# Row one-hots of a graph network's first norm: one broadcast comparison of two tensors, or 17 comparisons with a per-partition scalar

## The reference

```
h = relu(layernorm(x))                         # first norm
x = x + segment_sum(mlp(h[src], h[dst]), src)  # 128 -> 128 -> 128 -> 64, softplus
h = relu(layernorm(x))                         # second norm
z = relu((h + segment_sum(h[src], dst)) @ W1 + b1) @ W2 + b2
x = x + h + relu(batchnorm(z))
```

## Time and profile before

| | |
|---|---|
| three runs | 1983.5, 1985.07, 1986.97 us; median 1985.07 |
| the profiled execution | 1981.82 us, of which the span from first to last instruction is 1979.3 us |
| `prepare`, first `row_hot` to last | 82.17 to 289.41 us of the span, 49 blocks |
| DVE busy | 1063.9 us of the span, 3259 instructions |
| POOL busy | 1071.2 us of the span, 1151 instructions |
| PE busy | 1428.0 us |
| mean granted TensorE clock | 0.894 |

### The profile page before, as it was taken

One profiled execution on the slowest core, in us unless ns is written; L12 is line 12 of the kernel. 1 busy time (PEld: TensorE's weight loads), 2 busy tenths in 40 slices (PEclk: granted clock), 3 DMA queues, 4 the chain that ended last, 5 costly groups with the idle time before them and its releaser, 6 DMA issues. The chain is left out here.

```text
span 1979.3 us, 37799 instructions
## 1 busy us (share of the span) xinstructions
PE 1428.0 (72%) x10165; PEld 1067.5 (54%) x10165; DVE 1063.9 (54%) x3259; ACT 975.3 (49%) x2310; POOL 1071.2 (54%) x1151
## 2 busy tenths in 40 slices
PE   0033337999999999999999994666556556566566
PEld 0022225777777777777777784443434334334334
DVE  4899993555555555555555555443443433433344
ACT  0188885776777777677777763111111111111144
POOL 0388884454444445445444542776666666666600
PEclk9999999999999999999999997777777777777765
DMA  1255544444554554455455453222222222222259
GB/s 34 61 125 130 122 109 115 125 119 119 130 129 110 128 135 115 122 129 127 111 129 136 111 138 73 58 57 55 47 53 51 50 54 46 54 54 46 33 180 340
DMA packets 435913, 200.77 MB, mean 101 GB/s; under 512 B 382585, under 2 KB 408710, under 8 KB 435866
## 3 DMA queue, kind: packets, MB, share of 16 engines
q1 hardware_dynamic: 343384, 142.00, 27.7%
q0 software_dynamic: 28224, 32.57, 9.1%
q10 hardware_dynamic: 64258, 25.65, 4.5%
HBM read 131.49 MB, written 55.79 MB: 95 GB/s over the span
## 5 line engine op out<-in xcount | busy, mean ns | idle before, releaser
L821 POOL DMA_INDIRECT fast_gathered<-h_table,fast_gather_i x441 | 423.2, 960 | 471.8 <-PE bank L963 295.0
L1180 POOL DMA_INDIRECT fast_gathered<-h_neighbours_table,fast_index_i x441 | 425.8, 966 | 197.4 <-POOL fast_index_i L1176 104.9
L1080 ACT ACTIVATE fast_h<-bank,b_s 128x384 f32<-128x384 f32 (+1 forms) x490 | 299.7, 622 | 177.7 <-PE bank L990 140.4
L1241 PE MATMUL node_sums<-twice,fast_self_rows 128*64 128x128 f32 x784 | 139.0, 423 | 279.3 <-DMA fast_gathered<-h_neighbours_table,fast_index_i 275.2
L1241 PEld LDWEIGHTS node_sums<-twice,fast_self_rows 128*64 128x64 f32 x784 | 120.5, 222 | 317.5 <-issue 307.0
L1272 ACT ACTIVATE fast_z_in<-node_sums 128x512 f32<-128x512 f32 x49 | 29.3, 597 | 517.7 <-PE node_sums L1247 517.7
L1087 ACT ACTIVATE fast_h<-fast_h 128x384 f32<-128x384 f32 (+1 forms) x490 | 263.8, 558 | 0.0
L1226 DVE BATCH_NORM_STATS2 z_stats<-z_t (+1 forms) x48 | 33.3, 694 | 386.2 <-ACT z_t L1283 386.2
L999 PE MATMUL bank<-fast_h,w_s 128*128 128x384 f32 (+1 forms) x490 | 235.3, 562 | 2.8 <-ACT fast_h L1087 1.9
L1247 PE MATMUL node_sums<-fast_hot,fast_gathered 128*64 128x256 f32 (+1 forms) x980 | 217.4, 444 | 0.0
L1034 PE MATMUL node_sums<-fast_message,fast_hot 128*128 128x80 f32 x1568 | 200.9, 276 | 0.0
(11 more groups left out here) (234 smaller groups left out, 2578.9 us busy)
## 6 DMA issues: line engine op xcount, KB each, us to landing
fast_local<-local_rows SPq DMA_DIRECT2D x49, 576.0 KB, 5.5
h_neighbours_table<-fast_h_rows SPq DMA_DIRECT2D x49, 320.0 KB
fast_self_rows<-h_neighbours_table SPq DMA_DIRECT2D x49, 320.0 KB, 3.3
h_table<-prep_normed ACTq DMA_DIRECT2D x49, 256.0 KB, 2.7
fast_own_rows<-h_table SPq DMA_DIRECT2D x49, 256.0 KB
fast_own_cols<-h_cols SPq DMA_DIRECT2D x49, 256.0 KB
x_plus_h<-fast_total SPq DMA_DIRECT2D x49, 256.0 KB, 6.4
finish_resid<-x_plus_h SPq DMA_DIRECT2D x49, 256.0 KB, 4.0
```

The source lines that it names most:

```text
L821: pool.indirect_dma_start(gathered[slot][:, j * D:(j + 1) * D], None, h0_t, bass.IndirectOffsetOnAxis(ap=gather_i[q][:, n:n + 1], axis=0))\
L1080: A(to[at][:, 0:w], psum[:, 0:w], ACT.Exp, bias=b_s[:, :]).then_inc(done, 1)
L1180: pool.indirect_dma_start(gathered[q][:, c * MW:(c + 1) * MW], None, h1_t, bass.IndirectOffsetOnAxis(ap=index_i[q][:, c:c + 1], axis=0))\
L1241: nc.tensor.matmul(banks[6 + q % 2][h * D:(h + 1) * D, k * P:(k + 1) * P], self_rows[q][:, at:at + D], twice[:, :], start=(k == 0), stop=F ...
```

## The change

In `row_hots` the one comparison of two broadcast views (17 x 128 elements per partition) becomes 17 comparisons of `iota_h` (128 elements) with one number per partition, field 1 of the n-th edge. The result is the same tensor. The semaphore that tells of it moves to the last of the 17. Nothing else is changed, no wait and no DMA; 16 x 49 = 784 instructions are added on VectorE.

```diff
@@ -566,10 +566,10 @@
                                             iota_tile[:, bass.ds(b * CT, CT)].unsqueeze(1).to_broadcast([128, RAW, CT]),
                                             ALU.is_equal).then_inc(tile_hot_ready, 1)
                             wait_from(dve, pack_done, b - 1)
-                            V.tensor_tensor(groups(row_hot[q % 2][:, :], P),
-                                            f[:, :, 1:2].to_broadcast([128, RAW, P]),
-                                            iota_h[:, :].unsqueeze(1).to_broadcast([128, RAW, P]),
-                                            ALU.is_equal).then_inc(row_hot_ready, 1)
+                            for n in range(RAW):
+                                last = V.tensor_scalar(row_hot[q % 2][:, n * P:(n + 1) * P], iota_h[:, :],
+                                                       f[:, n, 1:2], None, ALU.is_equal)
+                            last.then_inc(row_hot_ready, 1)
```

## The result

The changed kernel took 2055.07 us (median of 4 runs, 2053.63 to 2055.91) against 1984.28 us before on the same chip (4 runs): a ratio of 1.0354, 95% interval 1.0336 to 1.0372, slower. The profiled execution took 2054.45 us, its span 2049.4 us.

The account below looks back on a forecast made before the run. VectorE was taken to set prepare's pace, 4.32 us a block, in a round with GpSimd where each waits for the other. +0.38 + 1.41 - 0.37 = +1.42 us a block, x 49 = +70 us, gave 2055 us, range 2000 to 2090.

Parts of the forecast that it names:

- The chain: In prepare, 17 comparisons at 0.16 us, 2.72 us, replace row_hot's 2.34: +0.38 us a block (-0.30 to +0.89).
- the two ends: Limits for one comparison in prepare: 0.12 us with elements free, 0.19 with elements as dear as four-byte ones.
- GpSimd gets in: Inside prepare's 17 comparisons, spread and centre get in and VectorE stands: +1.41 us a block.
- the first hold: In prepare, spread holds VectorE 0.84 us, less 0.12 fixed; centre's hold of 0.69 follows, with nothing taken off.
- Given back: In prepare, centre_rest no longer meets centre, falling from 0.65 to 0.28 us: -0.37 us a block.
- The sum: In prepare, +0.38 + 1.41 - 0.37 = +1.42 us a block, x 49 = +70 us.
- B: In prepare, GpSimd is kept out until the 17th comparison; only the chain is longer: 2004 us, chance 0.17.
- C: In prepare, the new comparisons share nothing with GpSimd, so no stall is left: 1985.5 us, chance 0.12.
- D: In prepare, the scalar's price vanishes (0.10 us each) and GpSimd is kept out or not met: 1960 us, chance 0.07.
- E: The change fails its purpose, for instance scalars 10 bytes apart cost another 0.06 us each: 2105 us, chance 0.04.

Follow-up runs that it names:

- the probe: Kernel before plus scratch-writing VectorE chains in setup, alone and beside GpSimd subtractions: 0.165 us per comparison with two-byte scalar; ten beside GpSimd took 2.37 us, not 1.63.
- the kernel before with the same wait: Kernel before, with GpSimd's spread made to wait until row_hot is through: 1997.6 us, ratio 1.006.

## Why the prediction was right

**The chain.** I forecast +0.38 us a block, and +0.42 was found (2.76 - 2.34): 0.1625 us from start to start where I took 0.16 from rows of four-byte numbers. No row had two-byte numbers in and out, so the middle between the two ends was a choice; it was right because the elements cost 0.033 us, as the probe shows. The probe also shows the scalar's load at 0.06 us. By the formula of the Trainium skill's page "VectorE: DVE Perf Modes", section "The TRN2 errata", the estimate is 0.094 us each. The probe agrees with it for a constant in the instruction (0.10 us) and not for a scalar per partition (0.163).

**GpSimd gets in.** I forecast +1.41, and +1.34 was found (0.71 for `spread`, 0.63 for `centre`). That these are meetings is shown from three sides: moving `centre` out shortens the chain by 0.61 us, reading from PSUM leaves no instruction above 348 ns, and the probe makes a stretch of 0.74 us with one GpSimd instruction beside a chain of ten. My split was a little off: I took 0.12 off the first hold and nothing off the second, and both came out shorter than the rows before had them (0.84 - 0.71 = 0.13, 0.69 - 0.63 = 0.06).

**Given back.** I forecast -0.37 for `centre_rest`, and -0.38 was found (0.65 to 0.27 us).

**The sum.** I forecast +1.42 a block, and 5.71 - 4.32 = +1.39 was found. `edges0` starts 66 us later and not 70: there are 48 rounds between the first and the last comparison and not 49, and the early ones cost less (5.13 us in place of 4.17 between the first two chains, +0.96). The median moved by 70.8 us: 66.2 from `prepare`, 4.0 from `finish`, 2.5 from outside the span, less 1.9 by which the two profiled executions differ from their medians. Only the 66.2 us come from what I forecast; `finish` is no work of the change, and what lies outside the span stays unexplained. The agreement of the total within 0.1 us (2055 and 2055.07) is thus partly luck; the sum per block was right to 2%, and the mechanism was as forecast.

**The rivals.** B (kept out until the 17th) falls with the trace: the third of 17 already stands. C (no meeting) falls for SBUF and would have held for PSUM. D's first condition, a price of 0.10 us, is met only by a constant. Nothing of E showed: a scalar from a field 10 bytes from the next costs 0.1625 us, one from a dense row 0.165.

The Trainium skill's page "SBUF — State Buffer", section "SBUF: two separate sides", states an exclusive lock between GpSimd and VectorE instructions in a two-port mode or with two SBUF inputs. No trace names the mode of an instruction, but the runs agree with the lock in all that was tried: a comparison of two SBUF tensors meets GpSimd (`spread` at 2.98 us in place of 0.97), and so does a one-tensor comparison of two-byte SBUF numbers (0.98 us in place of 0.24), while sums (0.67 us) and comparisons from PSUM (348 ns at most) do not.

## What to carry to other kernels

An instruction's duration can be waiting: where instructions of two engines meet, as VectorE's and GpSimd's do here, compare the instruction's end with the other engine's ends before costing it, and add up the held time of both engines. Cutting one long VectorE instruction into short ones lets GpSimd in between. The waiting then moves from GpSimd to VectorE, and here VectorE bounds the stage, so the time grows by it. Seventeen comparisons with a scalar per partition cost 17 x 0.13 us besides their elements. For a comparison of two broadcasts look first at the innermost steps: with steps of one it took 1.34 us in place of 2.41 here, for one copy of 17 numbers a block and a constant made once.

## What the runs showed of the hardware that was not expected

- Two two-byte tensors, one with an innermost step of five numbers: 2.73 us for 2176 elements, more than the 2.41 us with an innermost step of zero, and twice the 1.34 us with steps of one (rows of 17, an odd number, did not hinder that).
- TensorE's weight loads of the same slices with a step of 17 numbers took 161 ns on average in place of 104, their matmuls 219 in place of 187. TensorE was busy for 78 of 130 us there, and no wait of VectorE or ScalarE for it shows.
- GpSimd and VectorE instructions whose records start together: VectorE's next two got in first, and GpSimd's 0.83 us instruction took 1.20 us. In the kernel before with the same wait only the next one got in, and it took 0.97 us.
- A comparison of a four-byte PSUM row with a scalar per partition follows the one before after 0.26 us, with GpSimd at work beside it or not.
